# A windowed-attention block on one core: the 64-row products of FC1 put behind both bands' 128-row ones, and a new order of the transfers on SyncE

## The reference

```python
f = _ln(f, g1, b1)                                   # over the 96 channels
f = jnp.roll(f, (-3, -3), axis=(1, 2))
win = _window_partition(f)                           # 64 windows of 7 x 7 = 49 tokens
q, k, v = heads(win @ w_qkv + b_qkv)                 # 12 heads of 8
attn = softmax(q @ k.T * scale + mask)
out = (attn @ v) @ w_proj + b_proj
f = residual + roll_back(window_reverse(out))
m = _ln(f, g2, b2)
m = gelu(m @ w_fc1 + b_fc1) @ w_fc2 + b_fc2          # FC1: 96 to 192, FC2: 192 to 96
return f + m
```

## Time and profile before

| | |
|---|---|
| time, median of three runs | 2974.03 us |
| time of the profiled execution | 2974.94 us |
| its span, first to last instruction | 2973.1 us |
| busy share: PE, PEld, DVE, ACT, POOL | 96%, 80%, 81%, 69%, 59% |
| transfers: mean rate | 121 GB/s |
| median time to landing: high parts (147 KB), both parts (294 KB) | 2.1 us, 3.0 us |

### The profile page before, as it was taken

The page is one execution under the profiler, slowest core; times in us unless marked ns, Lnnn a source line. Parts: engine busy times, 40 slices in busy tenths (PEclk is TensorE's granted clock), DMA queues, the critical chain, the costliest instruction groups (busy, mean ns, idle before and its releaser), DMA issues.

```text
span 2973.1 us, 141485 instructions
## 1 busy us (share of the span) xinstructions
PE 2851.0 (96%) x54820; PEld 2383.1 (80%) x54820; DVE 2405.7 (81%) x7142; ACT 2036.8 (69%) x3208; POOL 1760.3 (59%) x2088
## 2 busy tenths in 40 slices
PE   3899999999999999999999999999999999999998
PEld 2788888888878888888887888888888788888886
DVE  6788887888888888788887888888888888888885
ACT  1677776677667777667766776767777677777674
POOL 3566566556656556565665566566565566666655
PEclk7999999999999999999999999999999999999999
DMA  3444444444445444444444444444444444444441
GB/s 72 126 123 126 130 121 126 121 125 126 126 118 130 125 129 123 120 125 123 125 129 114 124 127 125 125 123 125 130 122 126 121 124 130 127 121 129 122 113 42
DMA packets 414934, 359.65 MB, mean 121 GB/s; under 512 B 63646, under 2 KB 414176, under 8 KB 414204
## 3 DMA queue, kind: packets, MB, share of 16 engines
q1 hardware_dynamic: 414220, 350.04, 45.1%
HBM read 193.29 MB, written 154.14 MB: 117 GB/s over the span
## 4 chain that ended last, share of the span: by engine, by line
PE 89%; ACT 5%; issue 3%; DVE 2%; SPq 0%; DMA 0%; POOL 0%; DVEq 0%; POOLq 0%; ACTq 0%
PE psum L502 18%; PE psum L484 10%; PE psum L417 8%; PE psum L466 8%; PE psum L528 7%; PE psum L543 6%; PE psum L618 5%; PE psum L619 5%; PE psum L591 5%; PE psum L424 5%; ACT probs L678 4%; PE psum L428 3%; PE psum L581 3%; PE psum L445 2%; PE psum L570 1%
## 5 line engine op out<-in xcount | busy, mean ns | idle before, releaser
L678 ACT ACTIVATE probs<-psum 113x784 f32<-113x784 f32 x768 | 633.0, 824 | 639.1 <-PE psum L484 635.8
L796 DVE TENSOR_REDUCE nmax<-psum 113x16 f32<-113x784 f32 x768 | 745.5, 971 | 152.0 <-PE psum L466 151.6
L380 POOL TENSOR_SCALAR ve<-mv 98x8 f32<-98x8 f32 (+1 forms) x264 | 64.1, 243 | 1118.7 <-DVE mv L825 1085.9
L502 PE MATMUL psum<-vbd,probs 128*49 128x18 f32 x24576 | 642.5, 198 | 3.7 <-issue 3.0
L502 PEld LDWEIGHTS psum<-vbd,probs 128*49 128x49 f32 x24576 | 632.5, 126 | 6.7 <-issue 6.1
L387 POOL TENSOR_TENSOR rs<-ve,half 98x8 f32<-98x8 f32 (+1 forms) x264 | 435.3, 1649 | 0.0
L484 PE MATMUL psum<-qbd,kst 128*49 128x196 f16 x6144 | 401.5, 251 | 32.9 <-DVE xfl L831 21.9
L392 POOL TENSOR_TENSOR xn<-xn,rs 98x768 f32<-98x768 f32 (+1 forms) x264 | 383.3, 1452 | 74.5 <-POOL rs L387 74.5
L820 DVE BATCH_NORM_STATS2 st<-tok 98x6 f32<-98x96 f32 x2080 | 359.5, 246 | 71.3 <-ACT tok L685 56.4
L466 PE MATMUL psum<-kbd,qst 128*49 128x196 f16 x6144 | 399.2, 250 | 10.6 <-DMA kbd<-stack_pages 7.1
L383 POOL TENSOR_TENSOR xn<-tok,mv 98x768 f32<-98x768 f32 (+1 forms) x264 | 384.8, 1458 | 0.6 <-POOL ve L380 0.6
(11 more groups left out here) (90 smaller groups left out, 5716.3 us busy)
## 6 DMA issues: line engine op xcount, KB each, us to landing
stack_pages<-nat SPq DMA_DIRECT2D x256, 294.0 KB, 3.0
kst<-stack_pages SPq DMA_DIRECT2D x256, 220.5 KB
qbd<-stack_pages SPq DMA_DIRECT2D x1024, 55.1 KB
stack_pages<-nat SPq DMA_DIRECT2D x256, 147.0 KB, 2.1
xr<-in_x_dram SPq DMA_DIRECT2D x224, 147.0 KB, 3.2
out_dram<-yr SPq DMA_DIRECT2D x224, 147.0 KB, 2.3
qst<-stack_pages SPq DMA_DIRECT2D x256, 73.5 KB
kbd<-stack_pages SPq DMA_DIRECT2D x1024, 18.4 KB
```

The source lines that it names most:

```text
L502: last = nc.tensor.matmul(dst[:, :, h, :], probs[:, b.c % 2, h // 4, p, h % 4 * L:(h % 4 + 1) * L], vbd[:, b.c % 4, p * NH + h, :, :], sta ...
L678: nc.scalar.activation(probs[0:PR, b.c % 2, u, :, :].rearrange("j (g q) k -> j g (q k)", g=2), psum[0:PR, B:B + 2, 0:2 * CH], ACT.Exp).the ...
L796: nc.vector.tensor_reduce(dst, psum[0:PR, A:A + 2, 0:2 * CH].rearrange("i g (q h j) -> i g q h j", q=2, j=L), axis=AX.X, op=ALU.max, negat ...
```

## The change

FC1's function is split in two: `most` makes the 128-row products, `rest` the 64-row ones. TensorE's odd step now runs `most` of both bands, then `rest` of both. The semaphore `fc1_made` is raised after each `rest`. `back` in an odd step waits for the GELU of the first band alone (`HIDDEN[0]`), which is the one that reads bank B. On SyncE `save_parts` is split: the high parts of a band are written at the start of the next step's sequence and not at the end of this one's (between the two nothing else stood), followed by `load_x`, `maxima` and `key_blocks`; the stores and then both parts come behind, and `stacks` is last. No instruction is added or left out.

```diff
-            def save_parts(b):
+            def save_high(b):
                 n = b.c % 4
                 wait(sp, stack_in[n], b.step(-4).used(4, STACK_IN))
                 alone(sp)
                 sp.wait_ge(qk_high, b.count(1, 1))
                 alone(sp)
                 sp.dma_start(high_parts[n], nat[:, n, 0:4:2, :]).then_inc(high_out[n], 16)
+
+            def save_both(b):
+                n = b.c % 4
                 sp.wait_ge(qk_low, b.count(1, 1))
                 alone(sp)
                 sp.dma_start(both_parts[n], nat[:, n, :, :].rearrange("c (s m) t -> c s m t", s=2)).then_inc(nat_out[n], 16)
...
-                for offset, stage in ((LOAD, load_x), (KEYS, key_blocks)):
+                for offset, stage in ((QK - 1, save_high), (LOAD, load_x), (SCORE - 1, maxima), (KEYS, key_blocks)):
                     if has(t.step(offset)):
                         stage(t.step(offset))
                 if odd(t):
                     for offset in STORE:
                         if has(t.step(offset)):
                             store_y(t.step(offset))
-                for offset, stage in ((STACK, stacks), (SCORE, maxima), (QK, save_parts)):
+                for offset, stage in ((QK - 1, save_both), (STACK, stacks)):
                     if has(t.step(offset)):
                         stage(t.step(offset))
...
-            def most_and_rest(bank, high, low, b, kind):
+            def products(high, low):
+                return enumerate(((high, xfh), (high, xfl), (low, xfh)))
+            def most(bank, high, low, b, kind):
+                for n, (weights, tokens) in products(high, low):
+                    last = nc.tensor.matmul(three_parts(bank)[:, 0:2, :], weights[:, 0:FULL], tokens[:, b.c % 4, kind, :].rearrange("c (s t) -> c s t", s=2),
+                                            start=n == 0, stop=n == 2)
+                return last
+            def rest(bank, high, low, b, kind):
+                for n, (weights, tokens) in products(high, low):
                     for s in range(2):
                         last = nc.tensor.matmul(psum[REST * s:REST * (s + 1), bank + 1, 0:PART], weights[:, FULL:FULL + REST], tokens[:, b.c % 4, kind, s * PART:(s + 1) * PART],
                                                 start=n == 0, stop=n == 2)
...
-                    wait(pe, gelu_done, t.step(HIDDEN[1]).count(1, 1)) if has(t.step(HIDDEN[1])) else None
+                    wait(pe, gelu_done, t.step(HIDDEN[0]).count(1, 1)) if has(t.step(HIDDEN[0])) else None
...
-                last = most_and_rest((B, A)[n], w1h, w1l, b, 1)
-                last.then_inc(fc1_made, 1)
+                most((B, A)[n], w1h, w1l, b, 1)
+            def expand_rest(t, n):
+                b = t.step(HIDDEN[n])
+                if has(b):
+                    rest((B, A)[n], w1h, w1l, b, 1).then_inc(fc1_made, 1)
...
                     expand(t, 0)
                     expand(t, 1)
+                    expand_rest(t, 0)
+                    expand_rest(t, 1)
                     max_transpose(t)
```

## The result

The changed kernel takes 2937.06 us (median of 7 runs, 2933.94 to 2955.67) against 2974.03: ratio 0.9886, 95% interval 0.9866 to 0.9906. The forecast was 2935. The profiled execution took 2936.45, its span is 2934.7.

A forecast was written before the change was run, and what follows sets the result against it. TensorE, 89% of the chain of waits, bounds the kernel; 34 us from `back`'s earlier start plus 5 in the fill make 39 off 2974.94, 2936, predicted as 2935 for the median; 8-in-10 range 2915 to 2960.

The forecast's parts named there:

- What bounds: TensorE, 89% of the chain of waits; `back`'s "issue" wait is for the second GELU, 0.36 us in 126 odd steps.
- FC1's order: TensorE's odd step up to the max transpose: that transpose at 1.97 us after the first 128-row product, where it was 1.94.
- The stall and the saved changes of shape cancel: In FC1, a 0.20 us stall on VectorE's third maximum offsets 0.175 us saved by fewer changes of shape.
- the prediction's price of the changes: TensorE in FC1: a change of product shape costs 0.095 us one way, 0.08 the other; one of each saved, 0.175 a step.
- When `back` can start: Odd step: first GELU 1.78 to 2.44, `back` at 2.54 instead of 2.81; gain 0.27 us a step, 34 us over 126.
- What could take it back: Later in the step: ScalarE's work 0.30 to 0.39 later, `xfh` counted unchanged, 0.3 us left at the even step's second scores.
- The cover of 0.3 us: Even step's second scores: first maximum ends at 1524.03, TensorE's weight load comes at 1524.33; without cover each 0.1 us costs 12.6.
- SyncE: SyncE's new order: 0 in the regular steps (between -1 and +3 us), 5 us gained in the fill (between 0 and 7.1).
- The sum: Whole kernel: 34 + 5 = 39 us from the profiled 2974.94 gives 2936; predicted median 2935.
- No stall: Rival, FC1 in odd steps: maximum done in time, shape changes saved whole; 0.47 x 126 = 59, with fill 64, 2910; chance 0.08.
- Slower: Rival: stall on VectorE's third maximum delays both bands' 64-row products and GELUs; ending at 1.10 gives 2994 us; chance 0.05.

The follow-up runs named there:

- the wait alone: Kernel before with one word changed: `back` in an odd step waits for the first band's GELU, FC1's and SyncE's orders old; 2926.95 us, ratio 0.9860.
- the three pairs: Kernels differing in SyncE's order alone, old against new: kernel before 2973.15, 2973.06; with shorter wait 2926.95, 2927.70; fastest kernel 2896.71, 2894.68 us.
- two experiments: Changed kernel without the stall: VectorE's third maximum ahead of its division in odd steps, 2997.44 us; or FC1's 64-row products inside, 2909.55 us.

## Why the prediction was right

- **What bounds.** That the "issue" wait of `back` was the second GELU: shown by the wait alone, after which `back` follows the transposes by 0.39, the even step's figure.
- **FC1's order.** "The stall and the saved changes of shape cancel": max transpose at 1.90 (predicted 1.97, before 1.94), product behind the maximum at 0.67 (0.70), a stall of 0.18 (0.20) by the 0.495 of the kernel without it. The term was too dear by 0.07, since the 64-row pairs of both bands stand 0.09 apart and the wake-up took 0.05. The Trainium skill, TensorEngine Tiling (Array Packing), under Tiling Modes, says that a change of the tiling mode drains TensorE. The trace agrees: with one change each way less and no stall on the maximum, the max transpose comes at 1.72, 0.22 earlier than before, of which the prediction's price of the changes makes 0.175.
- **When `back` can start.** First GELU 1.76 to 2.42, `back` 2.52: predicted 1.78, 2.44, 2.54. Gain 0.28 a step for 0.27.
- **What could take it back.** Nothing did. ScalarE was mis-sized: the prediction lets the second GELU start when the first one ends, with all behind it 0.30 to 0.39 later. It starts 0.10 before that end (2.32 against 2.42), 0.27 later than before; the copy of the attention output comes 0.22 later (2.86 from the first product), the row of maxima 0.20, and `xfh` starts 0.11 before that row's end. So the 0.38 that was idle ahead of `xfh`, with this 0.11, just holds ScalarE's 0.20 and TensorE's 0.28: `xfh` (3.42) came 0.28 earlier, not at the same time, and VectorE's first maximum of the even step moved with TensorE. The cover of 0.3 us was never used. The thin place was elsewhere, at GpSimd's reordered rows, and I did not look there; it decides in some steps at 0.37 us a step (the wait alone), in nearly all at 0.60.
- **SyncE.** 0 in the steps and 5 in the fill: 5.2 in the trace. That these 5 us reach the time was the step that the runs don't bear out: in the three pairs SyncE's new order is 0.1 us faster, 0.8 slower and 2.0 faster. The traces have longer steps where the loop comes round, a place that the prediction did not name.
- **The sum.** 0.28 x 127 = 36, with the fill 41; the profiled time fell by 38.5. The six steps in which the loop comes round are 6.5 us longer than before in this trace, which is more than the difference. So the 2935 met the measured 2937 partly by luck: of its 39 us, the 34 of the wait were real and a little more, the 5 of the fill were not to be had in the time.
- **The rivals.** "No stall" is what two experiments made of it and not this change. "Slower" named the right place, the maximum; taken alone, FC1's order is slower, by 39 us.

## What to carry to other kernels

When an engine's busy share is 96%, look for the places where the same stage starts sooner in a sibling step: the difference, here 0.36 us, is a wait even if the profile gives it no name. A wait that is stricter than the buffer needs can cost time in every step that has it, and asking for a buffer earlier turns hidden slack into a stall, so weigh an order by when each operand is ready, not by the shapes alone. After each gain read which engine now ends last: here it was GpSimd, at 59% busy.

## What the runs showed of the hardware

Executions of one kernel differ by up to 0.7% (2933.94 to 2955.67). Six times in a run the loop comes round, and in the twelve traces these six steps are together 20 to 38 us longer than six median ones. Five stretches of the kernel before (the stretch, its length, busy time of PE, PEld, DVE, ACT and POOL with their instructions, PEclk as the granted clock, the transfers' share and GB/s):

```profile
1596.00:1600.00 4.00, 4.00 (x25) 3.41 (x23) 1.94 (x16) 2.10 (x5) 1.72 (x3) 1.00 0.66 155
1600.00:1604.00 4.00, 0.93 (x16) 0.60 (x16) 2.05 (x3) 0.00 (x0) 3.73 (x5) 1.00 0.11 20
1604.00:1608.00 4.00, 3.85 (x94) 3.72 (x90) 2.50 (x8) 1.74 (x3) 1.32 (x2) 0.59 0.30 83
1608.00:1612.00 4.00, 4.00 (x75) 3.71 (x71) 1.99 (x3) 1.39 (x2) 0.00 (x0) 0.50 0.32 79
...
1616.00:1620.00 4.00, 3.84 (x47) 2.80 (x47) 2.04 (x10) 3.19 (x7) 3.04 (x3) 1.00 0.15 37
```

TensorE is idle for some 3 us, then runs at a granted clock of 0.59 and 0.50 (0.50 is the lower level, 1.2 GHz), and is back at 1.00, 2.4 GHz, at 1616. This step is 7.27 us longer than the median one, that of another round of the same execution 2.49. A gain of 5 us hides in that.
